# Graph attention with pre-normalisation: prologue, last group and first-use waits rearranged

## What is computed

```
h     = relu(layernorm(x))              # x: (64, 128, 512) float32
out   = h @ W ;  q = h @ Wq ;  k = h @ Wk
alpha = relu(q @ k^T) * (adj != 0)      # 128 x 128 per graph
alpha = softmax(alpha, axis=1)          # over the first node index
y     = x + alpha @ out
```

## Time and profile before

| | us |
|---|---|
| median of 3 runs | 415.78 |
| lowest, highest | 415.6, 416.57 |
| the profiled execution, whole | 416.35 |
| the profiled span | 414.6 |
| PE busy | 404.2 (98%) |
| DVE busy | 296.5 (72%) |
| ACT busy | 277.5 (67%) |
| POOL busy | 259.7 (63%) |

### The profile page before, as it was taken

One profiled execution on the slowest core, in us unless ns is written; L12 is line 12 of the kernel. 1 busy time (PEld: TensorE's weight loads), 2 busy tenths in 40 slices (PEclk: granted clock), 3 DMA queues, 4 the chain that ended last, 5 costly groups with the idle time before them and its releaser, 6 DMA issues.

```text
span 414.6 us, 9426 instructions
## 1 busy us (share of the span) xinstructions
PE 404.2 (98%) x3571; PEld 320.8 (77%) x3571; DVE 296.5 (72%) x572; ACT 277.5 (67%) x589; POOL 259.7 (63%) x275
## 2 busy tenths in 40 slices
PE   5999999999999999999999999999999999999996
PEld 4444544879798797979889797979889797979983
DVE  4787689696767777686777678676777768656466
ACT  4489696486777776776767776677767677653523
POOL 0279887969486775939587685939577594920000
PEclk9999999999999999999999999999999999999999
DMA  8953758996969798896978699996988689393022
GB/s 285 370 106 75 207 101 203 224 222 175 188 199 199 243 127 215 203 216 173 194 240 149 167 209 227 186 196 205 169 250 167 166 209 233 40 183 115 2 102 103
DMA packets 161465, 75.03 MB, mean 181 GB/s; under 512 B 135312, under 2 KB 143504, under 8 KB 161424
## 3 DMA queue, kind: packets, MB, share of 16 engines
q1 hardware_dynamic: 160848, 73.42, 76.8%
q10 hardware_dynamic: 576, 1.05, 0.7%
HBM read 24.12 MB, written 16.78 MB: 99 GB/s over the span
## 4 chain that ended last, share of the span: by engine, by line
PE 80%; POOL 6%; DVE 5%; ACT 4%; DMA 3%; issue 1%; SPq 1%; DVEq 0%; ACTq 0%; POOLq 0%
PE bank L1063 10%; PE bank L1065 10%; PE bank L1066 10%; PE bank L1081 9%; PE bank L1080 9%; PE bank L1078 9%; PE s_bank L1094 3%; PE s_bank L1093 3%; PE s_bank L1092 3%; DMA x_sb<-in_x 2%; POOL hn_lo L387 2%; PE bank L1099 2%; PE bank L1100 2%; PE bank L1101 2%; ACT exps L585 1%
## 5 line engine op out<-in xcount | busy, mean ns | idle before, releaser
L387 POOL TENSOR_TENSOR hn_lo<-h,hn_hi 128x512 f16<-128x512 f32 x64 | 74.6, 1177 | 54.9 <-ACT hn_hi L503 54.8
L493 ACT ACTIVATE h<-x_sb,shift,rstd 128x512 f32<-128x512 f32 x64 | 49.8, 803 | 24.6 <-POOL shift L382 24.6
L413 POOL TENSOR_TENSOR hn_lo<-s,hn_hi 128x512 f16<-128x512 f32 x56 | 63.5, 1167 | 0.3 <-ACT hn_hi L508 0.3
L1065 PE MATMUL bank<-hT_lo,mt_hi 128*128 128x256 f16 x224 | 61.1, 273 | 0.0
L1066 PE MATMUL bank<-hT_hi,mt_lo 128*128 128x256 f16 x224 | 61.1, 273 | 0.0
L1063 PE MATMUL bank<-hT_hi,mt_hi 128*128 128x256 f16 x224 | 61.1, 273 | 0.0
L1078 PE MATMUL bank<-wt_hi,hT_hi 128*128 128x256 f16 x224 | 61.1, 273 | 0.0
L1081 PE MATMUL bank<-wt_hi,hT_lo 128*128 128x256 f16 x224 | 61.1, 273 | 0.0
L1080 PE MATMUL bank<-wt_lo,hT_hi 128*128 128x256 f16 x224 | 61.1, 273 | 0.0
L508 ACT ACTIVATE hn_hi<-s 128x512 f16<-128x512 f32 x56 | 33.7, 625 | 28.0 <-POOL s L402 22.1
L1063 PE MATMUL bank<-hT_hi,m_hi 128*128 128x256 f16 x168 | 45.8, 273 | 0.6 <-ACT bank L527 0.5
(11 more groups left out here) (140 smaller groups left out, 1091.2 us busy)
## 6 DMA issues: line engine op xcount, KB each, us to landing
x_sb<-in_x SPq DMA_DIRECT2D x16, 1024.0 KB, 5.6
out_h<-x_sb SPq DMA_DIRECT2D x64, 256.0 KB, 2.1
adj_sb<-in_adj SPq DMA_DIRECT2D x16, 256.0 KB, 5.3
w_sb<-in_L_gnn_weight SPq DMA_DIRECT2D x1, 1024.0 KB, 11.4
hn_lo<-in_L_gnn_wk ACTq DMA_DIRECT2D x2, 256.0 KB, 3.8
hn_lo<-in_L_gnn_wk SPq DMA_DIRECT2D x2, 256.0 KB, 3.6
hn_hi<-in_L_gnn_wq SPq DMA_DIRECT2D x2, 256.0 KB, 6.4
hn_hi<-in_L_gnn_wq ACTq DMA_DIRECT2D x2, 256.0 KB, 6.7
```

What stands on the lines that cost most here:

```text
L387: nc.gpsimd.tensor_tensor(hn_lo[:, s, b], h[:, b], hn_hi[:, s, b], ALU.subtract).then_inc(h_split, 1)
L413: nc.gpsimd.tensor_tensor(low, s32[:, f], high, ALU.subtract).then_inc(s_split, 1)
L493: nc.scalar.activation(h[:, b], x_sb[:, s, b], ACT.Relu, bias=shift[:, b:b + 1], scale=rstd[:, b:b + 1]).then_inc(h_made, 1)
L1065: nc.tensor.matmul(o, bh[:, k, cols], al[:, :, k], start=False, stop=False, skip_group_check=True)
```

## The change

It has these parts:

1. **Loads.** All four blocks of Wq are issued by SP, none by ACT. x of group 0 and W come in two halves each, with a semaphore per half.
2. **PE before the weights.** Twelve transposes of the identity (`WARM`) run as soon as it is made. The four blocks of Wk go into four PSUM banks, with no wait between them; ACT copies out blocks 0 and 2, DVE blocks 1 and 3 (`copy_wkT`, among the maxima of Wk). `product_m(0)` is cut in two around `transpose_wq(1)`, and one matmul pair instead of two of `product_m(2)` stands ahead of the small matmul.
3. **Scales.** W's maximum is taken in two halves. One step fewer leads to `w_scale` (it is formed by integer arithmetic from `pow2`, beside `ipow2`; the copy from PSUM is merged with the clamp), `m_scale` is made before the `w_lo`, and the statistics of group 1 all come after them. POOL makes the scales of group 0 for graphs 0 and 1 first (`first_scales`).
4. **Order in groups 0 to 3.** ACT: `exponentials(0)` behind `hi_of_h(2, ...)` of graphs 2 and 3; `hi_of_h(3, 1, 0)` directly behind the first `normalise_h(3, ...)`; `hi_of_whole_v(1, 3)` ahead of the sums of group 3. DVE: `lo_of_whole_t(1, 1)` and `(1, 2)` ahead of two or four of the statistics of group 3; `lo_of_wt(3)` moved back among the `lo_of_mt` and `lo_of_whole_v(1, ...)`. PE: the three waits ahead of group 2 become single waits at the first use of each part.
5. **Last group.** `lo_of_p` in two halves around `lo_of_v(LAST, 1, ...)`; the last graph's product, residual and store in two halves of 256 columns, in two banks.

The diff, cut to its core:

```diff
-    SCALE_STEPS = 8
+    SCALE_STEPS = 7
+    W_SHIFT = 12
+    WARM = 12
+        last_half = [bank[FREE][:, :HD], s_flat[:, :HD]]
+        wT_bank = [bank[k][:].rearrange("p (k n) -> p k n", k=K) for k in (VB, VE, VA, TE)]
...
-            for r in (0, 2):
+            for r in range(K):
                 sp.dma_start(wq_sb[:, r], wq[r * N:(r + 1) * N, :]).then_inc(wq_loaded[r], 16)
-            load_x(0)
-            sp.dma_start(w_sb[:], weight.rearrange("(k p) d -> p k d", p=N)).then_inc(w_loaded, 16)
+            for b in (0, HG):
+                sp.dma_start(x_sb[:, 0, b:b + HG], x_dram[:, b:b + HG, :]).then_inc(x0_loaded[b // HG], 16)
+            for k in (0, HK):
+                sp.dma_start(w_sb[:, k:k + HK], weight.rearrange("(k p) d -> p k d", p=N)[:, k:k + HK]).then_inc(w_loaded[k // HK], 16)
...
-            store(LAST)
+            for b in range(GB - 1):
+                sp.wait_ge(out_read, GB * LAST + b + 1)
+                sp.dma_start(out_dram[:, GB * LAST + b:GB * LAST + b + 1, :],
+                             x_sb[:, LAST % UNROLL, b:b + 1]).then_inc(stored[LAST % UNROLL], 16)
+            for f in range(2):
+                sp.wait_ge(out_read, B + f)
+                sp.dma_start(out_dram[:, B - 1, HD * f:HD * (f + 1)],
+                             x_sb[:, LAST % UNROLL, GB - 1, HD * f:HD * (f + 1)]).then_inc(stored[LAST % UNROLL], 16)
...
+            def first_scales(f):
+                c = slice(HG * f, HG * (f + 1))
+                pool.wait_ge(meanvar_made, HG * (f + 1))
...
-            for r in (1, 3):
-                act.dma_start(wq_sb[:, r], wq[r * N:(r + 1) * N, :]).then_inc(wq_loaded[r], 16)
...
-            for r in range(K):
+            for r in (0, 2):
                 act.wait_ge(wkT_filled, r + 1)
-                nc.scalar.activation(wkT[:, :, r], wT_bank[r % 2], ACT.Copy).then_inc(wkT_copied, 1)
+                nc.scalar.activation(wkT[:, :, r], wT_bank[r], ACT.Copy).then_inc(wkT_copied[r], 1)
...
-            exponentials(0)
             act.wait_ge(hT0_landed[2], 2 * 16)
             hi_of_h(2, 0, 2)
             hi_of_h(2, 0, 3)
+            exponentials(0)
...
             normalise_h(3, 3, 0)
+            hi_of_h(3, 1, 0, turn(0, 1))
             normalise_h(3, 3, 1)
             hi_of_whole_v(1, 1)
-            hi_of_h(3, 1, 0, turn(0, 1))
...
+            max_wk(0)
+            copy_wkT(1)
+            max_wk(1)
+            copy_wkT(3)
+            max_wk(2)
+            max_wk(3)
             for r in range(K):
                 vec.wait_ge(wq_loaded[r], 16)
                 weight_max(wq_sb[:, r], w_max[:, 1, r:r + 1])
             for b in range(GB):
-                stats_all(0, 0, b)
-            vec.wait_ge(w_loaded, 16)
-            weight_max(w_sb[:], w_max[:, 0])
+                stats_first(b)
+            for k in range(2):
+                vec.wait_ge(w_loaded[k], 16)
+                weight_max(w_sb[:, HK * k:HK * (k + 1)], w_max[:, 0, HK * k:HK * (k + 1)])
...
-            stats_all(1, 1, 0)
-            stats_all(1, 1, 1)
...
-            lo_of_wt(3)
-            for b in range(GB):
-                stats_all(3, 3, b)
             lo_of_whole_t(1, 1)
+            stats_all(3, 3, 0)
+            stats_all(3, 3, 1)
             lo_of_whole_t(1, 2)
+            stats_all(3, 3, 2)
+            stats_all(3, 3, 3)
             lo_of_whole_t(1, 3)
             for b in range(GB):
                 residual(0, 0, b)
+            make_mask(2, 0, 2)
             lo_of_mt(0)
+            lo_of_whole_v(1, 0)
             lo_of_mt(1)
-            lo_of_whole_v(1, 0)
+            lo_of_whole_v(1, 1)
+            lo_of_wt(3)
+            lo_of_whole_v(1, 2)
             lo_of_mt(2)
+            lo_of_whole_v(1, 3)
             lo_of_mt(3)
...
+            for k in range(WARM):
+                nc.tensor.transpose(top_bank[:, N * (k % K):N * (k % K + 1)], ident[:], ident[:])
             for r in range(K):
                 transpose_wk(r)
             transpose_wq(0)
+            product_m(0, range(2))
             transpose_wq(1)
-            product_m(0)
+            product_m(0, range(2, K))
...
-            pe.wait_ge(v_split, GB + TE + 1)
-            pe.wait_ge(mt_split, 4)
-            pe.wait_ge(wt_split, 4)
```

More of the change, by code:

```diff
@@ L191, in graph_attention_kernel @@
         stored = [sem(f"stored{s}") for s in range(UNROLL)]
-        w_loaded = sem("w_loaded")
+        w_loaded = [sem(f"w_loaded{k}") for k in range(2)]
         wq_loaded = [sem(f"wq_loaded{r}") for r in range(K)]
@@ L208, in graph_attention_kernel @@
         wqT_filled = sem("wqT_filled")
-        wkT_copied = sem("wkT_copied")
+        wkT_copied = [sem(f"wkT_copied{r}") for r in range(K)]
         wqT_copied = sem("wqT_copied")
@@ L434, in _ @@
             pool.wait_ge(consts_made, 5)
-            layernorm_scales(0)
+            first_scales(0)
+            first_scales(1)
             for b in range(GB):
@@ L526, in copy_p1_t @@
                 act.wait_ge(t_split, 4 * g)
+                if isinstance(g, int) and g == FIRST:
+                    act.wait_ge(v_split, GB + TB + 1)
                 nc.scalar.activation(bank[TB][:], bank[TA][:], ACT.Copy).then_inc(t_copied, 1)
@@ L732, in _ @@
             hi_of_h(3, 1, 3)
+            hi_of_whole_v(1, 3)
             hi_of_sum(3, 1, 0, S1)
             hi_of_sum(3, 1, 1, S3)
-            hi_of_whole_v(1, 3)
             hi_of_sum(3, 1, 2, S2)
@@ L841, in softmax_sum, with lo_of_p @@
                 nc.vector.reciprocal(row_inv[:], row_sum_s[:]).then_inc(inv_made, 1)
-            def lo_of_p(g):
-                for b in range(GB):
+            def lo_of_p(g, graphs=range(GB)):
+                for b in graphs:
                     vec.wait_ge(p_hi_made, GB * g + b + 1)
@@ L964, in _ @@
                                            pow2[:, 2:3], ALU.mult, ALU.mult).then_inc(scale_step, 1)
-            stats_all(1, 1, 2)
-            stats_all(1, 1, 3)
-            vec.wait_ge(scale_step, 6)
+            for b in range(GB):
+                stats_all(1, 1, b)
+            vec.wait_ge(scale_step, 5)
             for k in range(K):
@@ L1032, in _ @@
             lo_of_v(LAST, 0, bank[VA][:], 0, 0)
-            lo_of_p(LAST)
+            lo_of_p(LAST, range(HG))
             lo_of_v(LAST, 1, bank[VE][:], 0, 1)
+            lo_of_p(LAST, range(HG, GB))
             lo_of_v(LAST, 2, c22_v, 1, 1)
             lo_of_v(LAST, 3, bank[VB][:], 1, 0)
-            for b in range(GB):
+            for b in range(GB - 1):
                 residual(LAST, LAST % UNROLL, b)
+            for f in range(2):
+                vec.wait_ge(out_filled, B + f)
+                o = x_sb[:, LAST % UNROLL, GB - 1, HD * f:HD * (f + 1)]
+                nc.vector.scalar_tensor_tensor(o, last_half[f], out_unscale[:], o,
+                                               ALU.mult, ALU.add).then_inc(out_read, 1)
         @block.tensor
@@ L1113, in outs, with first_use @@
                 product_out(g, 3)
+            def first_use(g, split, f):
+                if g == FIRST:
+                    pe.wait_ge(split, f + 1)
             def period(i, j):
@@ L1173, in product_m @@
             def product_m(c, ks=range(K)):
-                pe.wait_ge(wkT_copied, K)
+                for r in range(K):
+                    pe.wait_ge(wkT_copied[r], 1)
                 pe.wait_ge(wqT_copied, c + 1)
@@ L1213, in _ @@
             nc.tensor.transpose(top_bank[0:3, 0:N], w_top[:], ident[:]).then_inc(top_filled, 1)
-            product_m(2, range(2))
+            product_m(2, range(1))
             pe.wait_ge(top_step, 3)
@@ L1217, in _ @@
             nc.tensor.matmul(top_bank[:, N:N + 3], ones[:], top_diag[:], start=True, stop=True).then_inc(top_filled, 1)
-            product_m(2, range(2, K))
+            product_m(2, range(1, K))
             product_m(3)
@@ L1296, in _ @@
                 pe.wait_ge(v_split, GB * LAST + (2 if b < HG else 4))
-                product_out(LAST, b)
+                if b < GB - 1:
+                    product_out(LAST, b)
+            for f in range(2):
+                dst, cols = last_half[f], slice(HD * f, HD * (f + 1))
+                nc.tensor.matmul(dst, p_hi[:, b], v_hi[:, b, cols], start=True, stop=False)
+                nc.tensor.matmul(dst, p_hi[:, b], v_lo[:, b, cols], start=False, stop=False)
+                nc.tensor.matmul(dst, p_lo[:, b], v_hi[:, b, cols], start=False, stop=True).then_inc(out_filled, 1)
 _INS = ["x", "adj", "L0_gnn_weight", "L0_gnn_wq", "L0_gnn_wk"]
```

84 lines of the change are left out of this document (52 added, 32 removed).

## The result

| | before | after |
|---|---|---|
| median, us | 416.45 (9 runs, 415.6 to 416.84) | 415.26 (9 runs, 414.45 to 415.73) |
| profiled execution, whole, us | 416.35 | 415.26 |
| span, us | 414.6 | 413.4 |

The ratio of after to before is 0.9972, with a 95% interval of 0.9964 to 0.9981: 1.2 us less (0.8 to 1.5). The three runs of before that stood ahead of the prediction had a median of 415.78; nine have 416.45, and the profiled execution, at 416.35, is typical of them.

What follows compares the result with a forecast made beforehand. TensorE, fully busy in the steady middle, was the bound, with POOL's group 3 chain bounding P2 of group 2. Gains of 1.45 and 0.15 made 1.6 us, taking the median from 415.78 to 414.1 us, range 413.0 to 415.9.

Steps and rivals of the forecast that it cites:

- DVE chain to the maxima: DVE's start: `w_top` at 17.0 instead of 17.34 us, 0.3 us won, first product with W at 24.8.
- Warm-up: Twelve PE transposes before Wk arrives: free within 0.1 us, about halving the Wk transposes, off the path.
- half of them fast: Eight Wk transposes before DVE's first copy: 1.3 us with half fast, 1.7 all slow; copy taken at 5.8.
- Wq by one issuer: Loads: Wq's first block lands a little before 7.7 us, DVE needs it at 8.9; costed at nothing.
- the cover: DVE's 1.15 us wait for Wq at the start, taken to absorb any lateness of Wq.
- Transposes of h: They land at 28.5 us, before PE asks at 30.0; the 0.28 us wait goes, gain 0.58 at 30.57.
- Groups 0 to 2: PE's waits before 64.89 and 75.66 go; POOL's chain puts P2 at 80.1 instead of 81.54, gain 1.45 us.
- The clash: Rival, chance 0.12: DVE's two-SBUF-operand instructions slow POOL's group 3 chain, 2.3 us added, P2 at 82.4, 416.5 us.
- the last group: End of the kernel: residuals no earlier, one more instruction costs 0.1, half store saves up to 0.35; gain 0.15 us.
- The level: Whole kernel: median of before taken as 415.78 us, 0.57 below the profiled execution, giving 414.1.
- All gaps close: Rival, chance 0.18: POOL's chain runs without DVE's interference and is no bound; PE gains 2.0 us, 413.4 us.
- The start gives nothing: Rival, chance 0.22: DVE reaches the weight maxima no earlier, 0.58 us lost, 0.85 + 0.15 left, 414.8 us.

Runs made afterwards that it cites:

- part 4 kernel: Kernel before with only the new orders in groups 0 to 3 and the waits at first use; 415.31 us in one execution, ratio 0.9983 over eleven runs.
- parts 1 to 4: Changed kernel with the whole last group put back as before, six runs; ratio to before 0.9959.
- two issuers: Changed kernel with blocks 1 and 3 of Wq issued by ACT again; 416.11 us in one execution.
- the kernel with the split `p_lo` only: Changed kernel keeping `lo_of_p` in two halves but with the last graph in one piece; 415.85 us in one execution.
- best: Changed kernel with the last group as before, group 3's fourth normalisation earlier on ACT, and DVE's second Wk maximum before its first copy; ratio to before 0.9933.
- second maximum first: Changed kernel with DVE's maximum of Wk block 1 ahead of its first copy; 414.79 us in one execution.
- halves alone: Changed kernel keeping the last graph in two halves but with `lo_of_p` in one piece; 414.78 us in one execution.

## Why the prediction was right in the middle and wrong at the end

- **DVE chain to the maxima**: 17.05 where 17.0 was forecast, the first product 24.93 for 24.8. The first copy was later than reckoned (6.15 for 5.8) and the statistics started, with that, at 11.51 for 11.5: the copies and the seven maxima cost 5.36 us for the 5.7 that I took. That the two totals fit within 0.15 us is partly luck: with the same start other executions had `w_top` between 16.56 and 17.05 and the first product between 24.44 and 25.62.
- **Warm-up**: called free and without effect on the path. It is off PE's path but not off DVE's: `copy_wkT` waits for the transposes. In the trace of after the chain of waits runs through the twelve. What it gives, 0.5 us on the second copy, was inside the forecast through "half of them fast"; that the moment of the fast pace would vary by 2 us between executions was not.
- **Wq by one issuer**: cost DVE nothing in after, and the cover held. The prediction reckoned with DVE only. PE takes Wq as soon as it is done with Wk (6.84 in after), and where it had to wait until 7.61 it reached `w_top` 0.5 us late.
- **Transposes of h**: no wait near 30. The part 4 kernel, without the early scales, still has it (0.37 us at 30.66 in one execution, 0.09 at 30.07 in the other).
- **Groups 0 to 2**: 0.43 and 0.30 us gone; sum at 71.14 for 71.0; copy of P1 at 79.47 for 79.46; P2 at 80.11 for 80.1. The distance from the first product, 55.18 for the 55.3 of the forecast, is steady and no luck. That the fourth `h` on ACT, behind `hi_of_whole_v(1, 2)`, is the gate was shown by moving it: P2 lost its gap.
- **The clash**: did not grow. POOL's first two sums took 1.27 and 1.28 us, not 1.7; the two low parts behind them took 2.72 where they had taken 2.26, so most of what the sums saved went there. Where the fourth `h` comes earlier the sums do take 1.44 and 1.73; that cost the chain 0.6 us and P2 nothing.
- **The failed step is the last group**: "DVE reaches the residuals no earlier: all its work ahead of them stays", and from it a gain of 0.15. The work stays, but I moved one piece ahead of its input: `v_lo` needs ACT's `v_hi`, which stands behind four `p_hi`, and the four `p_lo` had covered that. It measured -0.22. I had read DVE's timeline and not ACT's beside it. The half stores were to save up to 0.35; two half residuals and two half stores end no earlier than one whole (0.02 us later in this trace). The term was -0.24 in place of +0.15, an error of 0.39.
- **The level**: the forecast took 415.78 as the median of before, and more runs put it at 416.45, 0.67 higher. The forecast of the time missed by 1.16: 0.67 for this, 0.41 for the gain (1.6 against 1.19) and the rest rounding. With it 0.62 of the forecast's chances stood on a time under 414.5, and 415.26 is above that. The remark that the profiled execution lay 0.57 above the median should have been read as a doubt about a median of three.

Of the rivals, "All gaps close" did not come, since PE still waits 0.55 us at 80.11; what it supposed of POOL's speed came true in part, and wasn't the bound. "The start gives nothing" is refuted by part 4 alone (0.3 to 1.1 us) being worth less than parts 1 to 4 (1.2 to 2.2).

## What to carry to other kernels

Before an instruction is moved forward, look up what makes its input, on the other engine's timeline: work that stood ahead of it may be what hid the wait. A normalisation or copy that needs nothing from PE shouldn't stand behind one that does. Cutting the last piece in two pays only if the smaller last store saves more than the second instruction costs; here the second residual cost 0.15 us and the store gave about half of it back. And a start whose loads and pace vary by a microsecond has to be read from several executions, or from distances within one.

## What the runs showed of the hardware that I had not expected

- **A tiny DVE instruction that ends when POOL's does.** `top_diag` (3x3) took 0.22 us in part 4 alone, with POOL idle. The change starts POOL's `hn_lo` earlier, and beside it the same instruction took 0.48 us in after, 1.18 with two issuers and 1.22 in the kernel with the split `p_lo` only, where PE then waited 0.76 for it (DVE's row, POOL's four beside it, and the second of the four by itself):

```profile
17.93 1.22 DVE L976 TENSOR_SCALAR top_diag<-ident,top_col 3x3 f32<-3x3 f32 x1
```

```profile
16.75 4.71 POOL L406 TENSOR_TENSOR hn_lo<-h,hn_hi 128x512 f16<-128x512 f32 x4 [0.52 <-ACT hn_hi L521]
```

```profile
17.97 1.16 POOL L406 TENSOR_TENSOR hn_lo<-h,hn_hi 128x512 f16<-128x512 f32 x1
```

The length follows from the moment. In ten of the eleven traces with the new start `top_diag` ends within 0.03 us behind the end of one of POOL's `hn_lo`, each of which takes 1.16 us: it took 1.22 us where it began just ahead of the second (17.93 against 17.97), 0.48 in after, 0.25 in best, late in one. In the eleventh (second maximum first) it began 0.11 us before such an end and took its 0.22 us. The `pow` and `ipow` behind it (128x3) end in the same way. So a start one tenth of a microsecond later can cost a whole one. The clash that I had put at POOL's sums sits here too, and it is part of the spread between executions.

- **The first loads and the pace vary.** PE began with Wq between 6.67 (halves alone) and 7.84 us (two issuers) where the warm-up ran, and its transposes went over to the fast pace between 4.40 and 6.70 us, with the same twelve transposes from 1.58 us ahead of them.
- **A half store costs more than half an issue.** The two halves took 0.93 us on SP's queue, 0.47 each; three whole ones ahead of them took 1.65, 0.55 each.
- **A fixed part in the residual.** From start to start, 256 columns took 0.39 us, 512 columns 0.66: more than half.
